# A recurrent layer with expert tiles beside it: steps written out, other filler, an f16 projection, a middle buffer and later row scatters

## What is computed

```python
xW = einsum('ntd,dh->nth', x, Wx) + b          # x: 2 x 1024 x 256
h_t = tanh(xW_t + h_(t-1) @ Wh)                # 1024 steps, one after the other; h0 = cond
logits = h @ gate_w.T                          # 2048 tokens, 8 experts, the best 2 of each
probs = softmax(top2(logits))
y = sum over the two experts e of probs_e * ((silu(h @ wg_e.T) * (h @ wu_e.T)) @ wd_e.T)
out = x + y                                    # inner width 1024
```

## Time and profile before

| what | us |
|---|---|
| median of 3 executions | 1195.55 |
| lowest, highest | 1154.41, 1199.31 |
| the profiled execution | 1154.41 |
| its span, first to last instruction | 1152.2 |
| PE busy in it | 1115.8 (97%) |
| mean granted clock of PE | 0.744 |

### The profile page before, as it was taken

One profiled execution on the slowest core, in us unless ns is written; L12 is line 12 of the kernel. 1 busy time (PEld: TensorE's weight loads), 2 busy tenths in 40 slices (PEclk: granted clock), 3 DMA queues, 4 the chain that ended last, 5 costly groups with the idle time before them and its releaser, 6 DMA issues.

```text
span 1152.2 us, 42964 instructions
## 1 busy us (share of the span) xinstructions
PE 1115.8 (97%) x16126; PEld 759.0 (66%) x16127; DVE 454.5 (39%) x2369; ACT 453.3 (39%) x2730; POOL 92.7 (8%) x87
## 2 busy tenths in 40 slices
PE   9999999999999899999999899989999999999887
PEld 7666666666777676765777667766767767655554
DVE  3555556421444233432444333433243323452332
ACT  3455555422444333433444333433343324433332
POOL 0000000000101000100110100101010101011112
PEclk6555555555999857955999867985585757999999
DMA  4444444600010100000010101010100000311111
GB/s 115 129 122 137 134 133 134 205 11 16 17 21 17 23 12 16 22 12 18 17 26 17 28 7 21 17 23 16 21 17 11 17 6 19 95 34 23 25 26 23
DMA packets 36353, 51.36 MB, mean 45 GB/s; under 512 B 4497, under 2 KB 22802, under 8 KB 36114
## 3 DMA queue, kind: packets, MB, share of 16 engines
q1 hardware_dynamic: 29282, 39.37, 12.2%
q0 software_dynamic: 6864, 9.18, 4.9%
HBM read 34.90 MB, written 15.73 MB: 44 GB/s over the span
## 4 chain that ended last, share of the span: by engine, by line
PE 89%; DMA 5%; issue 3%; DVE 1%; ACT 1%; SPq 0%; POOLq 0%; ACTq 0%; DVEq 0%
PE bank L434 24%; PE bank L470 18%; PE bank L402 16%; PE bank L475 11%; PE bank L426 9%; DMA out<-y_sb,place_now 3%; PE bank L350 3%; PE bank L416 3%; PE bank L348 3%; DMA xrow<-expert_rows 2%; PE bank L391 1%; PE bank L514 1%; PE bank L378 0%; ACT y_sb L614 0%; SPq L239 0%
## 5 line engine op out<-in xcount | busy, mean ns | idle before, releaser
L470 PEld LDWEIGHTS bank<-hi,wh_hi 128*128 128x128 f16 x4096 | 267.7, 111 | 243.9 <-ACT hi L634 158.9
L634 ACT ACTIVATE hi<-bank 128x4 f16<-128x4 f32 x1024 | 179.4, 175 | 600.0 <-PE bank L475 598.9
L883 DVE TENSOR_TENSOR lo<-bank,hi 128x4 f16<-128x4 f32 x1024 | 166.9, 163 | 564.1 <-ACT bank L635 559.3
L434 PE MATMUL bank<-wh_hi 128*128 128x512 f16 (+3 forms) x970 | 348.9, 450 | 0.0
L470 PE MATMUL bank<-hi,wh_hi 128*128 128x2 f16 x4096 | 273.7, 171 | 13.4 <-issue 13.4
L475 PE MATMUL bank<-lo,wh_hi 128*128 128x2 f16 x4096 | 252.3, 165 | 0.0
L470 PE MATMUL bank<-hi,wh_lo 128*128 128x2 f16 x4096 | 247.5, 164 | 0.0
L402 PE MATMUL bank<-w_hi,x_T 128*128 x592 | 219.4, 428 | 4.5 <-issue 3.0
L470 PEld LDWEIGHTS bank<-hi,wh_lo 128*128 128x128 f16 x4096 | 181.9, 100 | 0.0
L475 PEld LDWEIGHTS bank<-lo,wh_hi 128*128 128x128 f16 x4096 | 179.9, 100 | 0.1
L635 ACT ACTIVATE bank<-bank 128x4 f32<-128x4 f32 x1024 | 173.3, 169 | 0.0
(11 more groups left out here) (120 smaller groups left out, 826.5 us busy)
## 6 DMA issues: line engine op xcount, KB each, us to landing
arena<-w_all SPq DMA_DIRECT2D x96, 256.0 KB, 2.7
xrow<-expert_rows SPq DMA_DIRECT2D x37, 132.0 KB, 2.1
expert_rows<-pad SPq DMA_DIRECT2D x32, 132.0 KB, 3.7
xt<-xT SPq DMA_DIRECT2D x16, 128.0 KB, 2.6
out<-y_sb,place_now POOLq DMA_INDIRECT x37, 3.8
expert_rows<-rows,slot POOLq DMA_INDIRECT x32, 2.6
arena<-wh_in SPq DMA_DIRECT2D x1, 256.0 KB
wx_sb<-wx_in SPq DMA_DIRECT2D x1, 256.0 KB
```

Source lines behind the costliest of these rows:

```text
L434: pe.matmul(bank[3][:, 0:min(n, 4) * P], wh_hi[:, 0, 0:P], wh_hi_cols[:, 0:min(n, 4) * P], start=True, stop=True, skip_group_check=True)
L470: pe.matmul(preact(i, tt)[:, B * m:B * m + B], w[:, k, m * P:(m + 1) * P], hi[:, pi, k, B * pt:B * pt + B], start=False, stop=False, skip_ ...
L634: act.activation(hi[:, i, :, B * tt:B * tt + B], src, ACT.Tanh, scale=1 / SCALE).then_inc(s_hi, 1)
L883: v.tensor_tensor(lo[:, i, :, B * tt:B * tt + B], h32[:, 4 * (tt % 2):4 * (tt % 2) + 4].rearrange("p (c b) -> p c b", c=2), hi[:, i, :, B ...
```

## The change

- The steps of all 16 blocks are written out on every engine, with waits on constants; the loop of the tail stays.
- `filler` chooses the filler by kind of step: none in blocks 0 to 3 but for 16 units in each of the last four steps of block 3; none beside gate and up; 4 beside the transposes; 1 (or the projection in its place) beside down; 8, 5 or 6 in the others.
- The projection is made of f16 parts: 12 matmuls per bank (three products of parts, two halves of x, two halves of the output), two in a step, in the steps of `XW_AT` that are all steps of down. The banks are not cleared but seeded with the bias. ACT splits x in step 22, DVE in step 23. x has one buffer in place of two.
- Place and weight go from `meta_in` through `meta_mid` (`pass_on`); SP's load of a tile waits for the take of the one before, and in the tail the take stands ahead of `all_lo` and `shift`.
- POOL's row scatters wait for a step: the first for step 37, the second for step 43 of the block.
- DVE's part of the weight split is one step later than ACT's, and ahead of the routing.

```diff
--- before.py
+++ after.py
...
+SCATTER_AT = (37, 43)
-XW_AT = ((19, 21, 23, 49, 51, 63), (18, 20, 22, 28, 48, 50))
+XW_AT = ((25, 27, 29, 31, 55, 57), (24, 26, 30, 32, 54, 56))
+X_HI_AT, X_LO_AT = 22, 23
+BURST_AT = (60, 61, 62, 63)
...
+        seed = sb("seed", [P, STEPS // 2, 2, B], F32)
-        xt = sb("xt", [P, 2, 2, P], F32)
+        xt = sb("xt", [P, 2, P], F32)
+        x_hi = sb("x_hi", [P, 2, P], F16)
+        x_lo = sb("x_lo", [P, 2, P], F16)
...
+        meta_mid = sb("meta_mid", [P, 2], F32)
...
+            def load_x(blk):
+                sp.wait_ge(s_xlo, blk)
+                sp.dma_start(xt[:], xT[:, :, blk * P:(blk + 1) * P]).then_inc(s_x, 16)
...
             def load_tile(q):
                 if not is0(q):
                     sp.wait_ge(s_xtp, q)
-                    sp.wait_ge(s_mt, 3 * q - 2)
+                    sp.wait_ge(s_take, q)
...
-                sp.wait_ge(s_sc, scattered)
-                sp.reg_add(scattered, scattered, 32)
+                sp.wait_ge(s_sc, 32 * blk)
                 load_tile(2 * (blk + 1 - FIRST))
...
-            with sp.Fori(FIRST // 2, PAIRS - 1) as pr:
-                for i in range(2):
-                    load_tile(2 * (pr * 2 + i - FIRST) + 1)
-                    load_x(pr * 2 + i, i)
-                    load_tile_a(pr * 2 + i)
+            for blk in range(FIRST, NBLK - 2):
+                load_tile(2 * (blk - FIRST) + 1)
+                load_x(blk + 2)
+                load_tile_a(blk)
...
+            def xw_mm(i, p, n):
+                m, k = n // 6, n // 3 % 2
+                w, xpart = ((wx_hi, x_hi), (wx_hi, x_lo), (wx_lo, x_hi))[n % 3]
                 dst = xw[p][:, i * P:(i + 1) * P].rearrange("p (t c b) -> p t c b", c=2, b=B)[:, :, m, :]
+                mv = xpart[:, k, :].rearrange("p (t a b) -> p t a b", a=2, b=B)[:, :, p, :]
+                return pe.matmul(dst, w[:, k, m * P:(m + 1) * P], mv, start=False, stop=False, skip_group_check=True)
...
+            def filler(blk, tt, tiles, last):
+                if not tiles:
+                    return 16 if blk == FIRST - 1 and tt in BURST_AT else 0
+                xw_too = not last and tt in XW_AT[0] + XW_AT[1]
+                if any(at <= tt < at + 12 for at in TILE_AT):
+                    return 0
+                if any(tt - at in TURN_AT for at in TILE_AT):
+                    return 4
+                if any(tt - at in DOWN_AT for at in TILE_AT):
+                    return 0 if xw_too else 1
+                return {0: 5, ROWS_TURN_AT[0]: 6, ROWS_TURN_AT[1]: 6, TURN_X_AT[0]: 5, TURN_X_AT[1]: 5}.get(tt, 8)
...
-                xw_too = not last and tt in XW_AT[0] + XW_AT[1]
-                if not tiles:
-                    keep_warm(6)
-                elif not any(at <= tt < at + 12 or tt - at in TURN_AT + DOWN_AT for at in TILE_AT):
-
-                    keep_warm({0: 5, ENTRY_AT[0]: 11, ENTRY_AT[1]: 9, ROWS_TURN_AT[0]: 6, ROWS_TURN_AT[1]: 6, TURN_X_AT[0]: 4, TURN_X_AT[1]: 3}.get(tt, 6 if xw_too else 8))
-                elif any(tt - at in TURN_AT for at in TILE_AT) and not xw_too:
-                    keep_warm(2)
+                keep_warm(filler(blk, tt, tiles, last))
...
-            pair(0)
-            pair(1)
-            with pe.Fori(FIRST // 2, PAIRS - 1) as pr:
+            for pr in range(PAIRS):
                 pair(pr)
-            pair(PAIRS - 1)
...
-                act.wait_ge(s_mt, 3 * q + 3)
+                act.wait_ge(s_mt, 2 * q + 2)
...
+                if not last and tt == X_HI_AT:
+                    act.wait_ge(s_x, 16 * (blk + 2))
+                    act.wait_ge(s_xw, blk + 1)
+                    act.copy(x_hi[:], xt[:]).then_inc(s_xhi, 1)
...
                 if not is0(q):
-                    v.wait_ge(s_mt, 3 * q)
-                v.tensor_copy(meta_in[:], xrow_meta).then_inc(s_mt, 1)
+                    v.wait_ge(s_mv, q)
+                v.tensor_copy(meta_in[:], xrow_meta).then_inc(s_take, 1)
+
+            def pass_on(q):
+
+                v.wait_ge(s_take, q + 1)
+                if not is0(q):
+                    v.wait_ge(s_mt, 2 * q)
+                v.tensor_copy(meta_mid[:], meta_in[:]).then_inc(s_mv, 1)
 
             def shift(q):
 
-                v.wait_ge(s_mt, 3 * q + 1)
+                v.wait_ge(s_mv, q + 1)
                 if not is0(q):
                     v.wait_ge(s_scat, 16 * q)
-                v.tensor_copy(place_now[:], meta_in[:, 0:1]).then_inc(s_mt, 1)
-                v.tensor_copy(weight_now[:], meta_in[:, 1:2]).then_inc(s_mt, 1)
+                v.tensor_copy(place_now[:], meta_mid[:, 0:1]).then_inc(s_mt, 1)
+                v.tensor_copy(weight_now[:], meta_mid[:, 1:2]).then_inc(s_mt, 1)
...
                 if tt == SHIFT_AT:
+                    pass_on(q)
                     shift(q)
...
-                if tt < 2:
-
-                    v.memset(xw[tt % 2][:, (1 - i) * P:(2 - i) * P], 0.0).then_inc(s_clr, 1)
+                if tt < 2 and not last:
+
+                    v.tensor_copy(xw[tt % 2][:, (1 - i) * P:(2 - i) * P], seed_cols).then_inc(s_clr, 1)
+                if not last and tt == X_LO_AT:
+                    v.wait_ge(s_xhi, blk + 2)
+                    v.tensor_tensor(x_lo[:], xt[:], x_hi[:], ALU.subtract).then_inc(s_xlo, 1)
+                if split_of(blk, tt - 1) is not None:
+                    split(split_of(blk, tt - 1))
...
             with v.Fori(FQ + 2, m + LEAST - 1) as q:
                 all_times_up(q)
+                take(q + 1)
                 all_lo(q)
                 shift(q)
-                take(q + 1)
+                pass_on(q + 1)
...
-            def scatter_rows():
+            def scatter_rows(blk):
 
                 pool.wait_ge(s_cp, 5)
                 pool.wait_ge(s_rt, routed)
                 for k in range(2):
+                    if blk < NBLK:
+                        pool.wait_ge(s_hi, blk * STEPS + SCATTER_AT[k] + 1)
                     pool.indirect_dma_start(rows_dram, bass.IndirectOffsetOnAxis(ap=slot[:, k:k + 1], axis=0),
                                             rows[:, k, :], None).then_inc(s_sc, 16)
...
-            with pool.Fori(FIRST, NBLK):
-                scatter_rows()
+            for blk in range(1, FIRST):
+                scatter_rows(blk)
+            for blk in range(FIRST, NBLK + 1):
+                if blk == NBLK:
+                    pool.wait_ge(s_fill, 32 * E)
+                scatter_rows(blk)
                 add_results()
                 add_results()
...
```

More of the change, by code:

```diff
@@ L463, in step @@
                 pi, pt = (i, tt - 1) if tt else (1 - i, STEPS - 1)
-                if tt in (2, 3):
-                    pe.wait_ge(s_clr, 2 * blk + tt - 1)
+                if not last and tt in (2, 3):
+                    pe.wait_ge(s_clr, 2 * blk + tt + 1)
                 pe.wait_ge(s_hi, n + 1)
@@ L509, in pair @@
                         step(pr * 2 + i, i, tt, **modes(pr, i))
-            pe.wait_ge(s_c, 3)
+            pe.wait_ge(s_c, 1)
+            for p in range(2):
+                mm = pe.matmul(xw[p][:, 0:2 * P].rearrange("p (a c) -> p a c", a=2), all1[:],
+                               all1[:].unsqueeze(1).to_broadcast([P, 2, P]), start=True, stop=True,
+                               skip_group_check=True)
+            mm.then_inc(s_bits, 1)
             for _ in range(56):
                 pe.matmul(bank[3][:, 0:P], all1[:], all1[:], start=True, stop=True, skip_group_check=True)
-            pe.wait_ge(s_prep, 2)
-            pe.wait_ge(s_x[0], 16)
+            pe.wait_ge(s_prep, 3)
+            pe.wait_ge(s_xlo, 1)
+            pe.wait_ge(s_clr, 2)
             for p in range(2):
-                for q in range(6):
-                    mm = xw_mm(0, p, q, start=(q == 0))
+                for n in range(12):
+                    mm = xw_mm(0, p, n)
             mm.then_inc(s_xw, 1)
-            pe.wait_ge(s_prep, 6)
+            pe.wait_ge(s_prep, 7)
             pe.wait_ge(s_cp, 5)
-            pair(0)
-            pair(1)
-            with pe.Fori(FIRST // 2, PAIRS - 1) as pr:
+            for pr in range(PAIRS):
                 pair(pr)
-            pair(PAIRS - 1)
             def all_gate_up(q, halves=(0, 1)):
@@ L652, in pair @@
                         step(pr * 2 + i, i, tt, **modes(pr, i))
+            act.wait_ge(s_x, 16)
+            act.copy(x_hi[:], xt[:]).then_inc(s_xhi, 1)
             act.wait_ge(s_w, 96)
@@ L657, in _ @@
             act.copy(hi[:, 1, :, P - B:P], h0[:]).then_inc(s_hi, 1)
-            pair(0)
-            pair(1)
-            with act.Fori(FIRST // 2, PAIRS - 1) as pr:
+            for pr in range(PAIRS):
                 pair(pr)
-            pair(PAIRS - 1)
             def all_silu(q):
@@ L905, in step @@
                     take(2 * (blk + 1 - FIRST))
-                if split_of(blk, tt) is not None:
-                    split(split_of(blk, tt))
             def pair(pr):
@@ L936, in _ @@
             v.wait_ge(s_hid, 1)
-            pair(0)
-            pair(1)
```

(7 more changed lines are left out.)

77 lines of the change are left out of this document (38 added, 39 removed).

## The result

The changed kernel takes **975.0 us** (median of four executions, 970.19 to 983.26); the kernel before, run beside it on the same chip, 1178.5 (four, 1154.41 to 1199.31). The ratio is 0.841 with a 95% interval of 0.832 to 0.851: faster by 15 to 17%. The profiled execution took 971.27 us, span 969.5, against 1154.4 and 1152.2.

A forecast was written before the change was run, and what follows sets the result against it. TensorE was taken as the bound, busy almost throughout, with filler and tile columns dear at the low clock. Terms summed to 982, 984 with 2.2 around the span; 21 for clock falls gave 1005 us, range 958 to 1095.

The forecast's parts named there:

- first tanh: Start of the kernel: 11.7 us as before, f32 matmuls swapped for two more splits, within 1.
- stop of step 58, block 15: Block 15: TensorE waits for a tile load behind SP's second-scatter wait and 16 pads, some 9.5 us.
- Part 1: Blocks 0 to 3 without filler: steps 0.96 to 0.79 us; three blocks 153 for 202, block 3 55 for 68.
- rival (c): Blocks 0 to 2: weight stream keeps 119 GB/s, blocks stay at 67 us, +48, total 1053; chance 0.10.
- Part 2: Loop turns at the ends of blocks 5, 7, 9 and 11 go: 4 x 3.5 = 14 us.
- Part 3: Tile blocks with f16 projection and filler by kind: denser steps hold the clock, 50.7 us each, twelve 608.
- Part 4: Row scatter waits: step 49 late by 0.7 us in twelve blocks, 8.4; block 15 stops some 9.5, plus 3.
- +0.79 to POOL's start: Tile blocks, row scatter chain: POOL starts the second scatter 0.79 us after the tanh of step 42 ends.
- The clock term: Tile blocks: the stop near step 48 brings the clock down in one block of four, 3 x 7 = 21 us.
- Rival (a): Tile blocks: clock falls in most after the stop, eight to twelve at 8 to 14 us, 1050 to 1150; chance 0.18.
- Rival (b): Step 48: no stop, POOL earlier or landing under 3.3, no falls; 975, or 963 with SP in time; chance 0.08.
- Part 5: Tail: take ahead of the shift removes TensorE's 7.8 us wait for tile loads, 140.9 to 133.

The follow-up runs named there:

- B: The kernel before the change, with its loop over pairs of blocks and f32 projection; 1178.5 us.
- e4: A with 6 units of filler in each step of blocks 0 to 3 except the burst's four; 965.5 us.
- A: The changed kernel itself, with the whole change applied to B; 975.0 us.
- e5: B with only its loop over pairs of blocks written out on PE, ACT and DVE; 1126.7 us.
- e3: A with B's old filler table in the tile blocks; 971.95 us.
- e6: e5 with A's filler and A's places of the projection, the projection still f32; 1018.7 us.
- e2: A with the second row scatter waiting for step 45 in place of 43; 1063.2 us.
- e7: A with one POOL register addition between the row scatter's wait and its indirect DMA; 976.2 us.
- e10: A with the tail's order of before: the next tile's take behind the low-part splits and the shift; 987.3 us.
- e8: A without the row scatters' waits in block 15 alone; 960.2 us.
- e11: A without row scatter waits, with 6 units of filler in each step of blocks 0 to 3 and no burst; 949.8 us.
- e9: A without the burst, the four steps of 2048 filler columns at the end of block 3; 971.4 us.

## Why the prediction was right, and where its steps were off

The forecast was 1005 us in a range of 958 to 1095; it came to 975.0, faster as forecast. Most terms were right within a few per cent. Against the profiled execution (971.3), whose terms stand below, it is 34 us too high, and 30 of them are three terms: the falls of the clock, the stops of step 49 and the tail.

| term | predicted | measured |
|---|---|---|
| first tanh | 11.7 | 9.6 |
| blocks 0 to 2 | 153 | 153.5 |
| block 3 with the burst | 55 | 55.2 |
| twelve tile blocks without stops | 608 | 607.7 |
| stops of step 49 | 8.4 | 3.0 |
| falls of the clock | 21 | 1.2 |
| stop of step 58, block 15 | 9.5 | 9.9 |
| cold steps behind it | 3 | 1.2 |
| tail | 133 | 128.2 |
| around the span | 2.2 | 1.8 |

**Part 1, blocks 0 to 3.** The size was right: 0.79 a step without filler and 55 for block 3. The reason beside it was not general. I read from block 0 that the filler earns nothing, and took the Trainium skill's rule (TensorE: Matmul & The Clock Gate, "Why this matters for your kernels"), keep TensorE busy, as contradicted. The row was true only of B, with its f32 projection and a clock that was at half before the first step. With the projection in f16 the same filler holds 1.00 (e4), and by the rule, which here agrees with the runs, it earns its keep: 9.5 us by the medians, 4.8 of it seen in blocks 0 to 3. The weight stream behaved as costed and better; rival (c) is answered by 172 GB/s.

**Part 2, the loop.** In A no block's end shows a pause, so the 14 us of the earlier trace rows are gone (step 63 is 0.78 in blocks 4 to 14). Taken alone on B the removal gave 62 us in the medians with wide scatter (e5); how much of that is the clock stays open.

**Part 3, projection and filler.** 50.7 per tile block was right (50.67 to 50.94 in the blocks whose stop stays under 0.2), and so was that the clock would hold. The reason was again mixed wrongly: I gave it to "denser steps". The square of e3, e5, e6 and A, with what else its rows differ in, points to the f16 projection, and shows the density idle beside it. In e5 and e6 the falls follow the f32 steps when these are moved; in A, e2, e3, e7 and e10 every fall of the tile blocks stands in steps 49 to 52, at the stop, or at the stop of step 58 in block 15.

**Part 4, the row scatters.** The queue was read rightly: second scatter, addition, landing, `place_now`, difference of step 49. The term that failed is "+0.79 to POOL's start", read from a result of the tail to its addition. Behind the tanh it took 0.28 (0.45 from the tanh's start, in block 5 as in ten others). With 0.5 us less, `place_now` starts at +5.44 to +5.83 in ten of twelve blocks. It is due at about +5.63, since a start at +5.73 made step 49 0.10 late (block 5) and one at +7.47 made it 1.85 late (block 12). So the stop becomes one that only a slow landing shows: 0.59 in block 11, 1.85 in block 12, at most 0.2 in the others. Why a result waits 0.77 for POOL (e10: ready at 891.64, DMA at 892.41) and a tanh's counter 0.28 isn't settled. It is not the tail or its loop: the additions at 269.6 and 320.4 in A's written-out steps start 0.77 behind their result too. An addition waits against a register's value, the scatter against a constant, and an instruction between wait and DMA makes no difference (e7). A scatter's wait against a register wasn't tried.

Block 15's stop was worked out as 9.5 and measured 9.87 (10.65 for step 58): SP's 16 pads 13.92 us, then the load. Dropping the wait there alone takes it away (e8).

**The clock term.** "One block of four" was too many (one fall in A's twelve blocks, 1.2 us for 21) since it hung on a stop in every block, and that A's one fall lasted three steps was luck: e7's behind a shorter stop lasted 20.5 us. The mechanism itself was right: with the stops made 1.4 to 2.3 us long it happens ten times in twelve (e2), and costs more than the stops. Between it goes either way: 1.10 brought a fall in e7 and 1.24 in e3, 1.53 none in e8, 1.85 one in A; up to 0.94 (e7, block 11) none came. Rival (a) is what A would have been two steps of scatter later: 1063, where I had given it 1050 to 1150. Rival (b) without the falls and with SP late was 975, the measured number, though the landing was not under 3.3 (it was 3.8 in the median): POOL came earlier, the other half of its condition.

**Part 5, the tail.** The mechanism was right, the size off: 12.7 in place of 8. I priced one row of waits, TensorE's for the load (7.8 us), and not what else the late load moved: in e10 ACT's copy of the turned rows and the first matmul of gate and up are late too, which shows as idle time under other names. The better row was the tile's own period: 10.34 against the 8.89 of a chain that is TensorE alone, 1.45 a tile and 13 for nine tiles.

**First tanh.** 24 f16 matmuls of 0.19 us, 0.9 us in all, in place of twelve f32 ones, which the profile shows as 24 of 0.27 to 0.47 us, 4.2 in all; the wait for the splits ahead of them (1.84) takes part of it back: 2.1 less, where I took 0 within 1.

## What to carry to other kernels

A hold-up of one engine is best read as a due time and an arrival: here `place_now` came within 0.2 us of its due time in most blocks, two steps more of delay cost 88 us by way of the clock, and no wait at all was 18 us better. When filler seems useless at the low clock, look first at what kind of matmul stands beside it and at whether the clock was up when the filler began, and test these apart before giving the credit to density. Price the removal of a wait in a loop by the loop's period against the bare chain of the next bound, not by the one row of waits that names it.

## What the runs showed of the hardware that was not expected

- **f32 matmuls and the clock.** Only in the kernels with the f32 projection did the clock fall out of a TensorE without idle time: at 10.07 in B (7.00 of 7.00 us busy before), at 923.8 in e5 (6.79 of 6.80), in steps 25 to 33 of e6 (8.00 of 8.00). With the same work in f16 and the same filler it was 1.00 from the first block to block 15's stop (e4) or to the end (e11). The Trainium skill, TensorE: Matmul & The Clock Gate, "Part 1: The HAM clock gate", ties the low clock to idle time. Of the falls in the tile blocks of the f16 kernels that agrees with the traces, all of them at a stop; of the falls with f32 it doesn't, nor of e2's 40.80 us at 0.50 with TensorE busy throughout. Whether it is f32 itself or its slower weight loads (0.19 us against 0.10) that counts isn't told apart.
- **Filler can hold a clock without being seen to raise it.** Without filler the clock fell within the first five steps of block 0 in A and its kin, TensorE being busy 35 of 50.9 us, and stayed low for 205 us until the burst or the tile blocks; with six units a step it never fell there (e4, e11).
- **A short stop can cost far more than itself.** Behind a stop of 1.10 us the clock fell in e7, behind one of 1.53 in e8 it didn't; the price was between 3 cold steps (A, 0.39 each) and a low stretch of 41 us (e2, from 440.3).
- **A released POOL starts its indirect DMA 0.28 us behind the semaphore of a tanh**, and 0.77 behind that of a result, in the steps as in the tail. In A an addition lands after 3.6 to 5.5 us, and the slow landings stood in much the same blocks from kernel to kernel: the longest step 49 is that of block 12 in A, e7, e8 and e10, of block 11 in e4, and of block 10 in e3 and e9.
